# Second attention of a two-layer kernel: slots of the exponentials counted on over chunks, and one root per head for half of the heads

## What is computed

```
diff_sq  = maximum(q_norm_sq + k_norm_sq - 2 q.k, 0)
denom    = maximum((1 - q_norm_sq) * (1 - k_norm_sq), 1e-6)
cosh_arg = maximum(1 + 2 * diff_sq / denom, 1)
distance = where(cosh_arg > 1, arccosh(cosh_arg), 0)
attn     = softmax(-distance);  out = attn @ v, then Wo, residual
```

## Time and profile before

| | |
|---|---|
| median of 3 runs | 3408.45 us (3400.47 to 3408.81) |
| profiled execution, its own time | 3408.97 us |
| span from first to last instruction | 3407.0 us |
| busy: PE, DVE, ACT, POOL | 87%, 65%, 55%, 26% of the span |
| mean granted TensorE clock | 0.841 |
| A1, loop of ScalarE's groups | 1805.5 to 2940.9 us of the span |

### The profile page before, as it was taken

One profiled execution on the slowest core, in us unless ns is written; L12 is line 12 of the kernel. 1 busy time (PEld: TensorE's weight loads), 2 busy tenths in 40 slices (PEclk: granted clock), 3 DMA queues, 4 the chain that ended last, 5 costly groups with the idle time before them and its releaser, 6 DMA issues. The chain is left out here.

```text
span 3407.0 us, 52574 instructions
## 1 busy us (share of the span) xinstructions
PE 2957.1 (87%) x17862; PEld 2174.2 (64%) x17862; DVE 2230.0 (65%) x5046; ACT 1884.4 (55%) x2052; POOL 875.3 (26%) x584
## 2 busy tenths in 40 slices
PE   4999968888769999799995888898888888589999
PEld 4888846666658888699994233343333333279998
DVE  5555557777645555666666677777777777366665
ACT  2222246767622222333433988989889899533333
POOL 1000010000000000100003566757656667310000
PEclk9999979998979999899996666666666666699999
DMA  2000000000000000100000000000000000100000
GB/s 81 0 0 0 0 1 1 0 0 0 0 1 0 0 0 2 48 0 0 0 0 0 1 0 0 0 0 0 0 0 0 0 0 0 50 1 0 0 0 25
DMA packets 3188, 17.98 MB, mean 5 GB/s; under 512 B 1088, under 2 KB 2112, under 8 KB 2112
## 3 DMA queue, kind: packets, MB, share of 16 engines
q1 hardware_dynamic: 3136, 17.32, 1.3%
HBM read 15.22 MB, written 2.10 MB: 5 GB/s over the span
## 5 line engine op out<-in xcount | busy, mean ns | idle before, releaser
L1404 POOL TENSOR_TENSOR A_Y<-A_Y,A_U 128x2048 f32<-128x2048 f32 x96 | 435.2, 4557 | 319.9 <-ACT A_U L1447 319.9
L1623 PE MATMUL ps<-A_QT,A_KT 9*128 9x512 f32 x512 | 288.3, 658 | 145.6 <-DVE A_U L1486 110.0
L140 POOL TENSOR_TENSOR rstd<-var_eps,half_neg 128x4 f32<-128x4 f32 x45 | 49.7, 1105 | 1209.1 <-DVE var_eps L120 1183.9
L1486 DVE SCALAR_TENSOR_TENSOR A_U<-ps,A_U 128x1024 f32<-128x1024 f32 x256 | 311.5, 1217 | 65.9 <-PE ps L1623 65.9
L1478 DVE TENSOR_SCALAR A_U<-ps 128x1024 f32<-128x1024 f32 x256 | 308.8, 1216 | 58.5 <-PE ps L1611 56.8
L1623 PEld LDWEIGHTS ps<-A_QT,A_KT 9*128 9x128 f32 x512 | 117.6, 284 | 297.2 <-DVE A_U L1486 236.1
L257 ACT ACTIVATE F1b_act<-ps 128x512 f32<-128x512 f32 x256 | 153.2, 598 | 246.9 <-PE ps L223 230.6
L257 ACT ACTIVATE F1a_act<-ps 128x512 f32<-128x512 f32 x256 | 153.2, 598 | 243.3 <-PE ps L223 226.9
L1595 PE MATMUL ps<-A_Y,A_VA 128*32 128x512 f32 x768 | 269.7, 839 | 15.5 <-ACT A_Y L1454 15.5
L1611 PE MATMUL ps<-A_QT,A_KT 28*128 28x512 f32 x512 | 259.1, 615 | 5.2 <-DVE A_U L1478 3.7
L257 ACT ACTIVATE F0b_act<-ps 128x512 f32<-128x512 f32 x160 | 95.6, 598 | 273.5 <-PE ps L223 273.5
(11 more groups left out here) (338 smaller groups left out, 6693.7 us busy)
## 6 DMA issues: line engine op xcount, KB each, us to landing
dn<-in_down SPq DMA_DIRECT2D x2, 2048.0 KB, 12.2
stage<-in_up SPq DMA_DIRECT2D x1, 2560.0 KB, 9.3
X<-in_x SPq DMA_DIRECT2D x1, 2048.0 KB, 7.8
F1a_up<-in_up SPq DMA_DIRECT2D x1, 2048.0 KB, 8.0
F1b_up<-in_up SPq DMA_DIRECT2D x1, 2048.0 KB, 7.4
out_x<-X SPq DMA_DIRECT2D x1, 2048.0 KB, 6.3
dn<-in_down SPq DMA_DIRECT2D x1, 1280.0 KB, 12.2
qkv_w_s<-in_w_qkv SPq DMA_DIRECT2D x2, 192.0 KB
```

Source lines behind the costliest of these rows:

```text
L1404: eng.tensor_tensor(flat(y_slot(h)), flat(y_slot(h)), flat(Um[:, h % UR]), ALU.add).then_inc(s["t_ready"], 1)
L1486: eng.scalar_tensor_tensor(out=u, in0=g_pair(), scalar=CLAMP, in1=u, op0=ALU.min, op1=ALU.mult).then_inc(s["u_ready"], 1)
L1623: last = eng.matmul(ps[:, 4 + b, :], KT[r:r + 9, h // 2, kt * P:(kt + 1) * P], QT[r:r + 9, h // 2, :], start=True, stop=True)
```

## The change

Slots of Y are counted on over the chunks: head h of chunk c uses number (16 c + h) % 6, with c taken modulo 3 (`m`) as 48 is a multiple of 6. So the loop's body is three chunks, and chunks 0 and 1 stand before it.

In each group, heads 0 and 1 are as before. For heads 2 and 3 VectorE computes u (u + 1) into the slot of Y (`square`, behind the burst), ScalarE takes one root of it in place, GpSimd adds u, and ScalarE runs ln(2y + 1) and exp(-1 ...).

```diff
-            SQUARED = ()
+            SQUARE_FROM = 2
...
-                def y_slot(h):
-                    n = h % YR
+                TURN = 3
+                def y_number(m, h):
+                    return (m * H + h) % YR
+                def y_slot(m, h):
+                    n = y_number(m, h)
                     return Y[:, n] if n < YR - 2 else y_more[:, n - (YR - 2)]
...
                     @block.scalar
                             for h0 in range(0, H, 4):
-                                for h in (h0, h0 + 1, h0 + 2):
-                                    joined = h == h0 + 2
-                                    y = y_two(h) if joined else flat(y_slot(h))
-                                    u = u_two(h) if joined else flat(Um[:, h % UR])
-                                    if h >= YR:
-                                        eng.wait_ge(s["pvh_done"], c * PAIRS + (h - YR) // 2 + 2)
-                                    elif not first and h < 4:
-                                        eng.wait_ge(s["pvh_done"], c * PAIRS + h // 2)
-                                    eng.wait_ge(s["u_ready"], c * HALVES + 2 * h + (4 if joined else 2))
+                                for h in (h0, h0 + 1):
+                                    y, u = flat(y_slot(m, h)), flat(Um[:, h % UR])
+                                    if not first or h >= YR:
+                                        eng.wait_ge(s["pvh_done"], c * PAIRS + h // 2 - 1)
+                                    eng.wait_ge(s["u_ready"], c * HALVES + 2 * h + 2)
                                     eng.activation(y, u, ACT.Sqrt, bias=1.0)
-                                    eng.activation(u, u, ACT.Sqrt).then_inc(s["s_ready"], 2 if joined else 1)
+                                    eng.activation(u, u, ACT.Sqrt).then_inc(s["s_ready"], 1)
+                                for h in (h0 + 2, h0 + 3):
+                                    y = flat(y_slot(m, h))
+                                    eng.wait_ge(s["y_ready"], c * (H // 2) + h0 // 2 + h - h0 - 1)
+                                    eng.activation(y, y, ACT.Sqrt).then_inc(s["s_ready"], 1)
                                 eng.preload_act_table_set("natural_log_exp_and_others")
-                                for h in (h0, h0 + 2):
-                                    y = y_two(h)
-                                    eng.wait_ge(s["t_ready"], c * H + h + 2 + UR)
-                                    eng.activation(y, y, ACT.Ln)
-                                    eng.drain()
-                                    eng.activation(y, y, ACT.Exp, scale=-2.0).then_inc(s["y_exp"], 2)
+                                y = y_two(m, h0)
+                                eng.wait_ge(s["t_ready"], c * H + h0 + 2 + UR)
+                                eng.activation(y, y, ACT.Ln)
+                                eng.drain()
+                                eng.activation(y, y, ACT.Exp, scale=-2.0).then_inc(s["y_exp"], 2)
+                                y = y_two(m, h0 + 2)
+                                eng.wait_ge(s["t_ready"], c * H + h0 + 4 + UR)
+                                eng.activation(y, y, ACT.Ln, scale=2.0, bias=1.0)
+                                eng.drain()
+                                eng.activation(y, y, ACT.Exp, scale=-1.0).then_inc(s["y_exp"], 2)
...
                     @block.vector
                             def burst(g, after):
                                 n0 = 8 * g
                                 relu(n0)
                                 for i in range(8):
                                     if i < 7:
                                         relu(n0 + i + 1)
                                     scale(n0 + i)
                                     after(i)
+                                square(g)
+
+                            def square(g):
+                                h0 = 4 * g + SQUARE_FROM
+                                eng.drain()
+                                if not first or h0 >= YR:
+                                    eng.wait_ge(s["pvh_done"], c * PAIRS + h0 // 2 - 1)
+                                for h in range(h0, 4 * g + 4):
+                                    u = flat(Um[:, h % UR])
+                                    eng.scalar_tensor_tensor(out=flat(y_slot(m, h)), in0=u, scalar=1.0, in1=u, op0=ALU.add,
+                                                             op1=ALU.mult).then_inc(s["y_ready"], 1)
...
+                        main(0, 0, True)
+                        main(1, 1, False)
+                        with eng.Fori(0, (B - 2) // TURN) as k:
+                            for i in range(TURN):
+                                main(TURN * k + (i + 2), (i + 2) % TURN, False)
```

More of the change, by code:

```diff
@@ L1176, in u_two @@
                     return Um[:, h % UR:h % UR + 2].rearrange("p n t q -> p (n t q)")
[L1178 to L1183, removed]
                 def flat(a):
@@ L1400, in _, with add, main @@
                         eng.sem_inc(s["rstd_ready"], 1)
-                        def add(c, h):
+                        def add(c, m, h):
                             eng.wait_ge(s["s_ready"], c * H + h + 1)
-                            eng.tensor_tensor(flat(y_slot(h)), flat(y_slot(h)), flat(Um[:, h % UR]),
+                            eng.tensor_tensor(flat(y_slot(m, h)), flat(y_slot(m, h)), flat(Um[:, h % UR]),
                                               ALU.add).then_inc(s["t_ready"], 1)
-                        def main(c, first):
+                        def main(c, m, first):
                             load_rows_gpsimd(eng, c)
@@ L1418, in main @@
                             for h in range(8, H):
-                                add(c, h)
+                                add(c, m, h)
                             if not first:
@@ L1487, in scale @@
                                                          op1=ALU.mult).then_inc(s["u_ready"], 1)
[L1488 to L1496, removed]
                             def burst(g, after):
@@ L1561, in _ @@
                             turned_vector(eng, 0, i, early_bank(i))
-                        main(0, True)
-                        with eng.Fori(1, B) as c:
-                            main(c, False)
+                        main(0, 0, True)
+                        main(1, 1, False)
+                        with eng.Fori(0, (B - 2) // TURN) as k:
+                            for i in range(TURN):
+                                main(TURN * k + (i + 2), (i + 2) % TURN, False)
                         out_copy_vector(eng, B - 1, 2)
@@ L1581, in _, with outputs @@
                         eng.sem_inc(s["pvh_done"], 1)
-                        def outputs(c, pair, kts):
+                        def outputs(c, m, pair, kts):
                             if kts[0] == 0:
@@ L1594, in outputs @@
                                     v0 = (kt * H + h) * VC
-                                    last = eng.matmul(ps[j:j + 32, OUT, :], VA[:, v0:v0 + 32], y_slot(h)[:, kt, :],
+                                    last = eng.matmul(ps[j:j + 32, OUT, :], VA[:, v0:v0 + 32], y_slot(m, h)[:, kt, :],
                                                       start=(kt == 0), stop=(kt == TPC - 1))
@@ L1598, in outputs, with main @@
                                 last.then_inc(s["pvh_done"], 1)
-                        def main(c, first):
+                        def main(c, m, first):
+                            before_m = (m + TURN - 1) % TURN
                             def difference(n):
@@ L1648, in turn_four, with pair_in_burst @@
                                 turn_tensor(eng, k, i0 + 3, WINDOW_BANKS[3])
-                            def pair_in_burst(n, pair, i):
+                            def pair_in_burst(n, m, pair, i):
                                 if i in (5, 6):
-                                    outputs(n, pair, (i - 5,))
+                                    outputs(n, m, pair, (i - 5,))
                                 if i == 7:
-                                    outputs(n, pair, (2, 3))
+                                    outputs(n, m, pair, (2, 3))
                             ahead(0)
@@ L1702, in main @@
                                 project_out_tensor(eng, c)
-                            outputs(c, 1, (0, 1, 2, 3))
-                            burst(2, lambda i: pair_in_burst(c, 2, i))
+                            outputs(c, m, 1, (0, 1, 2, 3))
+                            burst(2, lambda i: pair_in_burst(c, m, 2, i))
                             ahead(3)
@@ L1736, in _ @@
                         eng.wait_ge(s["turned"], EARLY)
-                        main(0, True)
-                        with eng.Fori(1, B) as c:
-                            main(c, False)
+                        main(0, 0, True)
+                        main(1, 1, False)
+                        with eng.Fori(0, (B - 2) // TURN) as k:
+                            for i in range(TURN):
```

(3 more changed lines are left out.)

28 lines of the change are left out of this document (11 added, 17 removed).

## The result

The changed kernel takes 3520.95 us in the median of 4 runs (3512.23 to 3521.55), the kernel before 3408.63 in the same comparison: 112.3 us more, a ratio of 1.0332 with a 95% interval of 1.0318 to 1.0346. The forecast was 3516 us, with a range of 3470 to 3560. The profiled execution took 3521.55 us, with a span of 3519.8. In its trace A1, from ScalarE's first table load in the stage to its first of the next, lasts 3102.76 - 1806.28 = 1296.5 us, before it lasted 2990.77 - 1805.52 = 1185.3: the loss lies in A1.

The account below looks back on a forecast made before the run. The prediction took the TensorE-VectorE chain, period 136.53 us a chunk, as the bound in A1. Slips of 8.74 plus holds of 5.1 made 13.8 us a chunk, times 7.75 chunks 107 us: 3516 us, range 3470 to 3560.

Parts of the forecast that it names:

- ScalarE follows: In A1 ScalarE follows the TensorE-VectorE chain; its 14.4 us less work and lost 8.1 us wait a chunk bring nothing.
- Where the squares start and what they move: Two 2.27 us squares start when their burst's last products end, pushing back VectorE's next work and making TensorE wait.
- the 8.74 us: Slips of VectorE's next work behind bursts 0 to 3: 2.30, 1.25, 2.71 and 2.48, summed per chunk.
- The holds: Squares meeting a GpSimd sum wait for its end: bursts 2, 3 and 0 by 2.6, 0.2 and 2.3, 5.1 us a chunk.
- The clock: TensorE's products after bursts 2 and 3 might run at 1.2 GHz after a gap: taken as 0, net 4.8 a chunk kept for the range.
- rival 2: Holds and a slower TensorE clock after the gap: 18.6 us a chunk, 3553 us; chance 0.22.
- Rival 1: Squares without a hold by GpSimd: only 8.74 us a chunk, 3477 us; chance 0.2.
- Rivals 3 and 4: Rival 3: ScalarE's group sets the pace, 3299 us, chance 0.05; rival 4: squares fit VectorE's idle time, some 3415, 0.04.

Follow-up runs that it names:

- experiment 1: Changed kernel without squares, heads 2 and 3 with their two joined roots again; counted slots and loop of three chunks stay: 3405.21 us, ratio 0.9994 to the kernel before.
- experiment 2: Changed kernel with each square cut from 2048 to 16 columns, ScalarE's one root reading u; waits stay: 3421.30 us, ratio 1.0040 to the kernel before.
- experiment 3: Changed kernel with GpSimd's sums of heads 0 and 1 of each group cut to 16 columns, squares whole: 3478.01 us, ratio 1.0207 to the kernel before.
- experiment 7: Changed kernel where GpSimd's sum of head 0 of each group waits for both squares of its group: 3516.06 us, ratio 1.0321 to the kernel before.
- experiment 6: Changed kernel with the squares moved from VectorE to GpSimd, as u times u without the + u: 3558.71 us, ratio 1.0446 to the kernel before.

## Why the prediction came out

**ScalarE follows.** Right, and shown by experiment 1: the counted slots end the wait at the chunk's head and the time stays. That 13.2 us less work on ScalarE (14.4 by the forecast) give nothing is shown by experiment 2, which has the one root without the squares' time; in the changed kernel ScalarE waits 7.7 to 12.1 us in each group of the rows above, where the forecast had some 7.

**Where the squares start and what they move.** Right. They took 2.28 to 2.29 us against 2.27, started with the end of the products, and TensorE's waits are those named: up to 4.9 us for the cast and 5.7 for V. Experiment 2 shows that it is their time and not their order that costs, experiment 3 shows the 8.74 us as 10.3 less 1.69, within 0.2, and burst by burst within 0.3.

**The parts, burst by burst.** The distance from the start of one pair of squares to the next was forecast by the old distance of the products' ends, plus slip and hold. From the rows of VectorE above and the four pairs after them (at 2351.43, 2385.43, 2425.57 and 2459.97):

| from the squares of | old + slip + hold | forecast | measured, two chunks | what differs |
|---|---|---|---|---|
| burst 0 | 38.39 + 2.30 + 2.3 | 43.0 | 40.74, 42.20 | hold 0.1 and 1.7 |
| burst 1 | 32.73 + 1.25 + 0 | 34.0 | 33.48, 34.00 | |
| burst 2 | 33.65 + 2.71 + 2.6 | 39.0 | 40.72, 40.14 | hold 2.8 and 2.3, products slower by 1.7 and 1.2 |
| burst 3 | 31.76 + 2.48 + 0.2 | 34.4 | 34.56, 34.40 | 36.11 from 2123.62, where the products took 5.32 |

**The holds: mechanism right, size too large.** Squares of bursts 2 and 0 are held and end after a sum, those of burst 1 never, as forecast; the 0.2 for burst 3 did not come. One row the forecast leaned on was a weak witness: L1355 has a single input tensor, so it is the held squares, not that row, that show the hold of two inputs. Burst 0's hold is 1.7 to 1.8 in four of six chunks and 0.1 to 0.2 in two. From the squares of burst 0 at 2006.19 to those at 2913.93 are six chunks; their holds sum to 21.8, 3.6 a chunk against 5.1.

**The clock: the term set to nothing.** I took 0 for it, as the rows showed no such gap, and kept 4.8 for the range. The 16 products behind burst 2 were slower than 3.63 in each of the six chunks, by 1.17 to 2.52, those behind burst 3 in two, by 1.69: 14.1 us in all, 2.4 a chunk. So the slow products of rival 2 came, at about half its price, and they did take a hold away: burst 0's is 0.1 where the products behind burst 3 had taken 5.32, for the squares then come after the sum. Slow products do not cost everywhere: behind burst 1 the 16 took 5.68 in two chunks, and the next squares came 33.5 us after those of burst 1, against 34.0 with 3.63. That the slow clock costs the 2.4 us rests on the rows of granted clock, on the table and on the sum below; no run changed it by itself. Nor is it shown what slows it: waits of 2.6 to 4.9 us went before all of these slow products, but 2.51 before fast ones in experiment 7.

**The sum.** 8.74 + 3.6 + 2.4 = 14.7 us a chunk; measured are (2913.93 - 2006.19) / 6 = 151.29, 14.8 more than 136.53. Times 7.75 that is 114.4, against 112.3 measured. The forecast of 13.8 a chunk had one term 1.5 too large and another 2.4 too small, so its closeness to the median, 5 us, is partly luck; that the 8.74 came out is not.

**The rivals.** Rival 1 (no hold) gave 3477, and experiment 3, which has no hold, 3478; that agreement is luck in part. In its trace six chunks, from the squares of burst 0 at 1994.14 to those at 2874.88, are 62 us longer than six of 136.53, where 8.74 a chunk make 52: the difference is about six slow products of 1.69. But A1 as a whole is only 3056.75 - 1801.65 - 1185.3 = 70 us longer, so what stands before and behind these six adds 8, where the forecast leaves 15. Rivals 3 and 4 fell: ScalarE's group is not the pace, and squares start behind the products, not behind the scale.

## What to carry to other kernels

Before work is moved off the fullest engine, see which engine's wait ends last in that stage: here 13 us a chunk taken from an engine at 92% were worth nothing, and 18 put on one at 75% cost nearly 15, holds and slow products included. Idle time counts only where the new work may stand: a square that waits for its slot stands behind the gap, not in it, and on GpSimd it closed a ring though a third of its time was free. And an operation on VectorE with both inputs in SBUF is to be planned with the sums of GpSimd beside it; putting the sum off only turned the hold into a wait.

## What the runs showed of the hardware that was not expected

The hold does not depend on the length of what is held: 16 columns lasted up to 3.96 us instead of 0.16, and a square that met the start of a sum of 4.51 lasted 6.57. By the Trainium skill, page "SBUF — State Buffer", section "Who interferes with whom", whoever issues first has the shared ports for its whole instruction and the other is blocked; the traces agree with these numbers. It goes the other way too: in the first chunk two sums and two squares took turns, two sums 11.06 us instead of 9.03 and two squares 10.47 instead of 4.49. The rows of GpSimd and VectorE for it:

```profile
1925.70 11.06 POOL L1402 TENSOR_TENSOR A_Y<-A_Y,A_U 128x2048 f32<-128x2048 f32 x2 [9.83 <-ACT A_U L1443]
```

```profile
1928.44 10.47 DVE L1512 SCALAR_TENSOR_TENSOR dn<-A_U 128x2048 f32<-128x2048 f32 x2 [2.34 <-PE ps L1605]
```

On GpSimd the product of a tile with itself took 3.60 us in the median of experiment 6, the sum of two tiles of the same size 4.54. And the chunk's length is not steady: from burst 0 to burst 0 it is 153.5, 149.5 and 150.7 us, and again so; in experiments 3 and 7, without holds and with the same loop of three chunks, each chunk has the same length within 0.2 us. So the loop alone does not make the cycle of three. Holds and slow products displace each other, as above; whether that alone makes it is open.
